# Attention by spans: the order of TensorE's products in a fused gated cross-attention and feed-forward kernel

## The reference

```python
b, ch, t_t = x.shape
h = N_HEADS
kc = ch // h
q = _proj(Wq, bq, x); k = _proj(Wk, bk, c); v = _proj(Wv, bv, c)   # einsum('oc,bct->bot') + bias
q = _rope(q, d_rope); k = _rope(k, d_rope)
scores = jnp.einsum('bhqd,bhkd->bhqk', q, k) / jnp.sqrt(jnp.float32(kc))
p_attn = jax.nn.softmax(scores, axis=-1)
out = jnp.einsum('bhqk,bhkd->bhqd', p_attn, v)
return _proj(Wo, bo, out)

x = x + jnp.tanh(g_xattn[0]) * xattn(_layernorm(x), ctx)
x = x + jnp.tanh(g_ffn[0]) * ffn(_layernorm(x))   # fp4 weights, 512 -> 1408 gated by silu -> 512, rms norm
```

## Time and profile before

| | us |
|---|---|
| median of 3 runs | 727.04 |
| lowest, highest | 726.96, 729.21 |
| the profiled execution | 727.19 |
| its span | 725.4 |

### The profile page before, as it was taken

One profiled execution on the slowest core, in us unless ns is written; L12 is line 12 of the kernel. 1 busy time (PEld: TensorE's weight loads), 2 busy tenths in 40 slices (PEclk: granted clock), 3 DMA queues, 4 the chain that ended last, 5 costly groups with the idle time before them and its releaser, 6 DMA issues.

```text
span 725.4 us, 13353 instructions
## 1 busy us (share of the span) xinstructions
PE 689.1 (95%) x4660; PEld 334.3 (46%) x4660; DVE 611.1 (84%) x825; ACT 521.4 (72%) x925; POOL 476.5 (66%) x403
## 2 busy tenths in 40 slices
PE   3579999999999999999999999999999999999995
PEld 1234434443444344434443444656565556555653
DVE  6599989888988898888889779766899789977894
ACT  2028888888888888888888876665666566666653
POOL 2946555786678667866633129876697669766773
PEclk9559999999999999999999999999999999999999
DMA  6877777787777877877663202000001000100011
GB/s 206 219 184 168 180 197 190 175 184 205 201 173 178 216 184 182 201 197 190 166 150 70 85 24 74 1 1 0 1 1 44 15 1 0 45 16 0 4 42 72
DMA packets 48935, 80.59 MB, mean 111 GB/s; under 512 B 14436, under 2 KB 17892, under 8 KB 48868
## 3 DMA queue, kind: packets, MB, share of 16 engines
q1 hardware_dynamic: 47568, 78.73, 42.6%
q10 hardware_dynamic: 1300, 1.01, 0.5%
HBM read 45.11 MB, written 32.24 MB: 107 GB/s over the span
## 4 chain that ended last, share of the span: by engine, by line
PE 52%; POOL 26%; issue 14%; DVE 4%; DMA 2%; ACT 1%; SPq 0%; POOLq 0%; ACTq 0%; DVEq 0%
PE pv_ps L845 20%; POOL probs L300 15%; PE s_ps L815 14%; PE st_ps L827 9%; POOL probs L304 9%; DVE max_rows L1113 2%; PE st_ps L800 2%; PE st_ps L857 2%; PE st_ps L788 2%; PE st_ps L794 2%; POOL over_stack L224 1%; DMA xt_all<-x_dram 1%; DMA image<-split_rest 1%; DMA qk_stack<-image 1%; ACT probs L950 0%
## 5 line engine op out<-in xcount | busy, mean ns | idle before, releaser
L1113 DVE TENSOR_REDUCE max_rows<-s_ps 128x2 f32<-128x1024 f32 x256 | 305.2, 1212 | 44.9 <-PE s_ps L815 44.1
L950 ACT ACTIVATE probs<-st_ps 128x512 f32<-128x512 f32 x512 | 277.6, 596 | 63.8 <-PE st_ps L827 53.0
L319 ACT ACTIVATE probs<-s_ps,gu_sc 128x512 f32<-128x512 f32 x176 | 117.7, 685 | 84.4 <-PE s_ps L405 84.2
L300 POOL TENSOR_TENSOR probs<-probs 128x512 f32<-128x512 f32 x88 | 120.3, 1371 | 69.4 <-ACT probs L319 69.0
L845 PE MATMUL pv_ps<-probs,v_all 128*32 128x256 f32 x2048 | 163.2, 391 | 2.2 <-ACT pv_all L956 2.2
L815 PE MATMUL s_ps<-qk_stack 48*128 48x512 f32 x512 | 133.7, 519 | 8.4 <-DVE max_rows L1113 7.4
L171 DVE SCALAR_TENSOR_TENSOR proj<-s_ps,gu_sc,proj 128x512 f32<-128x512 f32 x132 | 98.7, 748 | 11.1 <-PE s_ps L405 1.9
L827 PE MATMUL st_ps<-qk_stack 50*128 50x512 f32 x512 | 108.0, 411 | 0.0
L421 PE MATMUL st_ps<-dn_head,over_input 128*128 128x512 f32 x264 | 104.9, 423 | 1.0 <-DVE over_input L182 1.0
L815 PEld LDWEIGHTS s_ps<-qk_stack 48*128 48x128 f32 x512 | 49.7, 191 | 115.8 <-issue 71.7
L845 PEld LDWEIGHTS pv_ps<-probs,v_all 128*32 128x32 f32 x2048 | 40.6, 108 | 97.8 <-ACT probs L950 81.3
(11 more groups left out here) (120 smaller groups left out, 883.6 us busy)
## 6 DMA issues: line engine op xcount, KB each, us to landing
qk_stack<-image SPq DMA_DIRECT2D x60, 384.0 KB, 6.2
image<-split_head SPq DMA_DIRECT2D x31, 256.0 KB
image<-split_head SPq DMA_DIRECT2D x62, 128.0 KB
image<-split_rest SPq DMA_DIRECT2D x31, 256.0 KB
xt_all<-x_dram SPq DMA_DIRECT2D x16, 256.0 KB, 4.0
ct<-ctx_dram SPq DMA_DIRECT2D x16, 256.0 KB, 3.4
scale_of<-inverse_scratch SPq DMA_DIRECT2D x16, 256.0 KB
out_dram<-over_stack SPq DMA_DIRECT2D x16, 256.0 KB, 2.0
```

The source lines that it names most:

```text
L300: nc.gpsimd.tensor_tensor(pair[:, n], parts[T_ % 2][:, 2 * n], parts[T_ % 2][:, 2 * n + 1], ALU.add).then_inc(pairs_ok, 1)
L319: nc.scalar.activation(parts[T_ % 2][:, k], gu_ps[(2 * k) % BANKS], ACT.Copy, scale=gu_sc[:, k, T_ % IT:T_ % IT + 1]).then_inc(gate_read, 1)
L950: nc.scalar.activation(probs[at % PROBS][:, tile % 4, :], st_ps[item % ST_BANKS][:], ACT.Exp).then_inc(st_read, 1)
L1113: nc.vector.tensor_reduce(out, s_ps[item % S_BANKS][:], AXIS_X, ALU.max).then_inc(s_read, 1)
```

## The change

TensorE's step is written by spans. A span now issues: the weighing of its first slot, the scores of both slots, the weighing of its second slot, then what belongs to the span (both projections in span 1; V and the mixing in span 2), then both halves of the values of the span before. `transposed_items` and ScalarE's `scalar_step` follow the same order, and the values now run exactly one span behind, so the last half before the feed-forward's loop is gone from there. The inputs turned in step 15 go to spans 6 and 7, two after each.

```diff
--- before.py
+++ after.py
@@ -47,12 +47,12 @@
 SPANS = QUADS * KT
 ST_BANKS, S_BANKS = 3, 2
 X_TILES, C_TILES, PROBS = 8, 4, 3
-MIX_AT, ROT_AT, PASS_AT, V_AT, INVERT_AT = 5, 2, 3, 11, 9
+WHOLE_AT, PROJECT_AT, INVERT_AT = 2, 1, 9
 AHEAD_PROJ = 3
 
 IMG_ROWS, K_ROW0 = 102, 49
 GROUPS = B // GROUP
-FIRST_TURN, TAIL_AT = 12, 3
+FIRST_TURN, TAIL_AT = 6, 3
 BANKS = 4
 NT = (B // GROUP) * IT
 LAG = 2
@@ -78,15 +78,13 @@
             items.append(("v", 0))
         items += [("rot", n), ("pass", n)]
     for b in range(B):
-        for slot in range(SLOTS):
-            if slot == V_AT and b + 1 < B:
+        for span in range(SPANS):
+            items += [("weight", b, tile) for tile in range(4 * span, 4 * span + 4)]
+            if span == PROJECT_AT and b + AHEAD_PROJ < B:
+                items += [("rot", b + AHEAD_PROJ), ("pass", b + AHEAD_PROJ)]
+            if span == WHOLE_AT and b + 1 < B:
                 items.append(("v", b + 1))
-            items += [("weight", b, 2 * slot), ("weight", b, 2 * slot + 1)]
-            if slot == ROT_AT and b + AHEAD_PROJ < B:
-                items.append(("rot", b + AHEAD_PROJ))
-            if slot == PASS_AT and b + AHEAD_PROJ < B:
-                items.append(("pass", b + AHEAD_PROJ))
-            if slot == MIX_AT and b >= 2:
+            if span == WHOLE_AT and b >= 2:
                 items.append(("mix", b - 2))
     items += [("mix", B - 2), ("mix", B - 1)]
     return items
@@ -857,28 +855,30 @@
                 nc.tensor.matmul(out, wo[:], heads_out[:], start=True, stop=True).then_inc(st_full, 1)
 
             def tensor_step(pe, b):
-                for slot in range(SLOTS):
+                for span in range(SPANS):
+                    slot = 2 * span
+                    weigh(pe, b, slot)
                     if b + 1 < B:
                         score(pe, b + 1, slot)
-                        if slot == V_AT:
-                            project_v(pe, b + 1)
-                    weigh(pe, b, slot)
-                    if slot == ROT_AT and b + AHEAD_PROJ < B:
+                        score(pe, b + 1, slot + 1)
+                    weigh(pe, b, slot + 1)
+                    if span == PROJECT_AT and b + AHEAD_PROJ < B:
                         project_rot(pe, b + AHEAD_PROJ)
-                    if slot == PASS_AT and b + AHEAD_PROJ < B:
                         project_pass(pe, b + AHEAD_PROJ)
-                    if slot == MIX_AT and b >= 2:
+                    if span == WHOLE_AT and b + 1 < B:
+                        project_v(pe, b + 1)
+                    if span == WHOLE_AT and b >= 2:
                         mix(pe, b - 2)
-                    if slot >= 3:
-                        values(pe, b, (slot - 3) // 2, (slot - 3) % 2)
-                    elif slot == 0 and b:
-                        values(pe, b - 1, SPANS - 2, 1)
-                    elif b:
-                        values(pe, b - 1, SPANS - 1, slot - 1)
-                    if b == B - 1 and FIRST_TURN <= slot < FIRST_TURN + KT:
-                        if slot == FIRST_TURN:
+                    for part in two:
+                        if span:
+                            values(pe, b, span - 1, part)
+                        elif b:
+                            values(pe, b - 1, SPANS - 1, part)
+                    if b == B - 1 and span >= FIRST_TURN:
+                        if span == FIRST_TURN:
                             pe.wait_ge(s_read, B * SLOTS)
-                        ffn["turn_inputs"](pe, 0, slot - FIRST_TURN)
+                        for k in (2 * (span - FIRST_TURN), 2 * (span - FIRST_TURN) + 1):
+                            ffn["turn_inputs"](pe, 0, k)
 
             def tensor_feed(pe, T_):
                 g, t = divmod(T_, IT)
@@ -925,7 +925,6 @@
                 pe.wait_ge(gu_turned, BIT_STEPS)
                 for n in two:
                     ffn["gate_up"](pe, 0, n)
-                values(pe, B - 1, SPANS - 2, 1)
                 for part in two:
                     values(pe, B - 1, SPANS - 1, part)
                 for T_ in range(NT + LAG):
@@ -977,21 +976,20 @@
                                      scale=keep["gates"][:, 0:1]).then_inc(st_read, 1)
 
             def scalar_step(act, b):
-                for slot in range(SLOTS):
-                    if slot == 3 and b:
+                for span in range(SPANS):
+                    for tile in range(4 * span, 4 * span + 4):
+                        exponential(act, b, tile)
+                    if span == PROJECT_AT and b + AHEAD_PROJ < B:
+                        for w in two:
+                            bias_half(act, b + AHEAD_PROJ, w)
+                    if span == WHOLE_AT and b + 1 < B:
+                        take_v(act, b + 1)
+                    if span == WHOLE_AT and b >= 2:
+                        gate(act, b - 2)
+                    if span == 0 and b:
                         values_out(act, b - 1, 1)
-                    if slot == 11:
+                    if span == KT:
                         values_out(act, b, 0)
-                    if slot == V_AT and b + 1 < B:
-                        take_v(act, b + 1)
-                    for odd in two:
-                        exponential(act, b, 2 * slot + odd)
-                    if slot == ROT_AT and b + AHEAD_PROJ < B:
-                        bias_half(act, b + AHEAD_PROJ, 0)
-                    if slot == PASS_AT and b + AHEAD_PROJ < B:
-                        bias_half(act, b + AHEAD_PROJ, 1)
-                    if slot == MIX_AT and b >= 2:
-                        gate(act, b - 2)
 
             @block.scalar
             def _(act):
```

## The result

The changed kernel takes 742.71 us in the median of 4 runs (741.58 to 749.83); the kernel before took 727.0 beside it (726.6 to 729.21, 4 runs). The ratio is 1.0231, with a 95% interval of 1.02 to 1.0263: slower, as forecast, but by 15.7 us and not by 27. The range of 746 to 766 doesn't hold it. The profiled execution took 743.24 us, its span is 741.4, 16.0 above that of before.

A forecast was written before the change was run, and what follows sets the result against it. TensorE was taken as the bound, with a ring through ScalarE's exponentials and three st_ps banks just as long. 1.61 a step over 15 steps (24.2) plus 2.6 for step 15 gave +26.8 on 727.19: 754.0 us, range 746 to 766.

The forecast's parts named there:

- the ring: ScalarE's exponentials and three st_ps banks: a span's fourth tile waits for the first's bank, starting at 1.19 us.
- the stand: TensorE waiting before a span's fourth tile until the first tile's exponential ends: 0.43 us.
- two unknowns: Passage between the values halves and cost of step 0; they set the range, 746 to 766 us.
- The span: Two slots of an attention step: 2.66 us against 2.47 before, eight times, +1.49 a step.
- V and mixing: Products in span 2: 1.09 and 1.06 us, plus a 0.07 wait for the second tile's bank.
- Projections, copies, turning: Per step: projections 2.03 less about 0.05 plus a 0.07 wait; copies of values +0.12; turning of maxima +0.09.
- All steps the same: One growth of 1.61 us taken for each of the 15 steps with scores, step 0 included: 24.2.
- Step 15: Last step, without scores: +3.8 us from its spans, less a shorter stand and tail, +2.6.
- (1): Rival: drains saved and the first tile's bank free in time, 42 us less, 685 us; chance 0.03.
- (2): Rival: VectorE's ring of maxima decides, 2.44 us a span, +0.5 a step, 735 us; chance 0.03.
- (3): Rival: VectorE's extras, some 3 us a step, aren't absorbed: 45 us more, 799 us; chance 0.05.
- (4): Rival: waits in each span lower TensorE's granted clock, over 850 us; chance 0.02.

The follow-up runs named there:

- e8_mix_apart: The changed kernel with the mixing moved to span 3, one span later and apart from V: 745.34 us (ratio 1.0251).
- e2_half_max: The changed kernel with each VectorE maximum taken over 256 of 512 keys: 740.11 us (ratio 1.0167).
- e7_tiny_exp: The changed kernel with exponentials over 8 of 512 columns after the first three spans and maxima over 256 of 512 keys: 696.98 us (ratio 0.9586).
- e1_half_exp: The changed kernel with exponentials over 256 of 512 columns after the kernel's first three spans: 732.93 us (ratio 1.006).
- e11_cover_gone: The kernel before with its other products in other slots (projections 5 and 6, mixing 8, V 14): 744.73 us (ratio 1.0242).
- e9_v_mix_behind: The kernel before with V and then the mixing side by side behind the weighing of slot 11: 733.14 us (ratio 1.0082).

## Why the prediction was wrong, point by point

The sign, the ring and the place of the stand were right. What failed is the sum: 1.61 a step was forecast, and laid on all 15 steps alike; a full step grew by 0.87, and the short ones 1, 13 and 14 by 1.05, 0.4 and 0.75. With smaller terms beside it that made the total too large by 10.8 us, and the range, which hung on two unknowns only, was too narrow at its lower end.

- *The span.* Forecast 2.66, measured 2.61. The ring's part holds: fourth tile at 1.19 (measured 1.18), values at 1.62 (1.61). The mis-sized term is the values, 1.04 for 1.00: the first to the second pass is 0.24, the last to the next shape 0.33, as taken, so the two passages between take 0.43 together, not 0.47. Eight times, 0.4 a step.
- *V and mixing.* Forecast 1.09 + 1.06 + 0.07, measured 4.62 - 2.61 = 2.01. I carried both prices over from places where a change of shape and an exposed load stood beside each, though I had just read that such a change costs 0.2 with its load. `e8_mix_apart` confirms the size, 0.26. 0.2 a step. (The 1.09 was also too low for V's old place: the sum of 4.36 before has 1.28 for it.)
- *Projections, copies, turning.* Span 1 is 4.64, 2.03 above a span; forecast 2.05 + 0.09. The turning costs nothing there: the second score waits to 252.88, but in `e2_half_max`, where it doesn't, span 1 is 4.63 as well. 0.1 a step. Of the two copies, only the one before span 5 costs, 0.09; the one before span 1 falls under the projections. 0.03.
- *All steps the same.* 1.61 was laid on 15 steps. But a step without projections had been 22.73 before, not 24.15 - 2.03 = 22.1, because in the old order too they covered waits: its span 1 without them is 3.07, with a plain span of 2.48. So steps 13 and 14 grew by 0.4 and 0.75 alone, and step 1, short by the mixing, by 1.05: 2.6 less than forecast together. Step 0 grew by 3.2 less the 1.0 of an earlier start, 0.6 or 0.7 more than forecast. The rows of these steps were in the trace of before.
- *Step 15* with the tail: forecast +2.6, measured +1.9.

Taken together, over the 11 full steps 0.74 x 11 = 8.1, the short steps 2.6, step 0 -0.6 and step 15 0.7: 10.8, the distance from +26.8 to +16.0.

The rivals: (1) didn't come, and `e7_tiny_exp` makes its condition true: with the bank free in time a step is 21.5. The Trainium skill's rule (TensorEngine Tiling (Array Packing), section Key Properties), that a change of tiling mode drains TensorE, agrees with that kernel: the old order's step is 24.10 and the new one's 21.52 when nothing else holds them. Of the 2.58 between them about 0.3 is V and the mixing side by side. An estimate from the other 2.3 is 0.14 us for each of the 16 changes between row products and column products that a step is spared; the runs show their sum, not how a single one comes about. (2) and (3) fell with `e2_half_max`: halving VectorE's work changes no full step (steps 13 and 14 by 0.08). `e1_half_exp` shows that (2) is next in line, where (3)'s extras add to it. (4) didn't come: the granted clock is 1.00 from step 1 on.

What stays open is the start. The trace places step 0's 3.2: its span 1 takes 7.96 for 5.56 at a mean granted clock of 0.55 for 0.67, and the other spans add the rest, as in later steps. Both projections now fall ahead of the rise of the clock, at 57.1, where their passes are about 0.9 us apart; before, it rose at 54.5, as the second projection began, whose passes are 0.48 apart. In `e2_half_max`, of the same order, the span takes 7.98 and the clock rises at 54.7, again near the span's end. Why it rises when it does was not tried.

## What to carry to other kernels

Grouping products of one shape spares TensorE its changes, but it also draws the writes of a ring of banks together; ask how long each bank is held by its reader (here 1.18 us from the write's start) and what TensorE has left to do in that time (here 0.81, as `e7_tiny_exp` shows; the forecast had 0.76). Before moving a product, ask what it covered where it stood (two copies of the values in `e11_cover_gone`, 1.1 us a step), and price it from a place with the neighbours it will have. Where steps differ, read each kind of step, not the typical one times their number.

## What the runs showed of the hardware that wasn't expected

In the changed kernel's block of values (245.56 to 246.56) the passes start 0.240, 0.215 and 0.216 us apart: the passage from one half to the other is as short as the one within the second half, and only the first is longer. The mixing behind V takes 0.95 from its first pass to the next shape, where it took 1.06 alone. And a stand of TensorE can cost more than its length: in `e9_v_mix_behind` it has nothing to do for 5.5 us, and the granted clock is 0.50 for 13.6 us from within that stand on.
